# Gated cross-attention and mixture-of-experts blocks, one core: the stages before the first expert layer put in another order

## The reference

```python
def depool(h, ctx_n):
    s = scan(s = a * s + b * ctx_n[:, :256])
    return s[plug] + h

h = rmsnorm(layernorm(x)) * g_res @ W_in + b_in
x = x + tanh(g_xattn[0]) * depool(h, rmsnorm(ctx) * g_init)
x = x + tanh(g_ffn[0]) * moe_top1(layernorm(x))
x = x + tanh(g_xattn[1]) * attention(layernorm(x), ctx)
x = x + tanh(g_ffn[1]) * moe_top2(layernorm(x))
```

## Time and profile before

| | us |
|---|---|
| three runs of the kernel before: median | 1360.92 |
| lowest and highest | 1360.55, 1364.99 |
| the profiled execution, its own time | 1368.55 |
| its span, first to last instruction | 1366.8 |
| busy in the span: PE, PEld | 1180.5, 863.4 |
| busy in the span: DVE, ACT, POOL | 520.4, 465.5, 479.6 |
| mean granted TensorE clock | 0.932 |

### The profile page before, as it was taken

How to read it: one execution, slowest core, us unless ns; L and a number is a source line. 1 busy time by engine, 2 the same in 40 slices (tenths; PEclk the granted TensorE clock), 3 DMA queues, 4 the chain that set the end, 5 groups by cost and what they waited for, 6 DMA issues and landing times.

```text
span 1366.8 us, 19293 instructions
## 1 busy us (share of the span) xinstructions
PE 1180.5 (86%) x7110; PEld 863.4 (63%) x7110; DVE 520.4 (38%) x1256; ACT 465.5 (34%) x1067; POOL 479.6 (35%) x496
## 2 busy tenths in 40 slices
PE   2466799999995889999999999999948999998986
PEld 2246699999993444545445454434438888888875
DVE  1574322221114796767667676522060010000100
ACT  2111122221110245555555555663302333333331
POOL 0150111111113156767557675580002333333322
PEclk9885699999996689999999999999957999999998
DMA  6114487878862000000000000012005999999984
GB/s 202 50 62 154 170 292 277 292 291 305 325 251 100 0 1 1 1 17 1 1 1 17 1 1 16 9 39 101 0 0 196 317 306 315 294 308 302 330 299 124
DMA packets 53978, 197.18 MB, mean 144 GB/s; under 512 B 8539, under 2 KB 34397, under 8 KB 38013
## 3 DMA queue, kind: packets, MB, share of 16 engines
q1 hardware_dynamic: 39584, 173.35, 35.7%
q0 software_dynamic: 10464, 18.36, 5.5%
q10 hardware_dynamic: 3836, 4.24, 1.0%
HBM read 179.54 MB, written 16.38 MB: 143 GB/s over the span
## 4 chain that ended last, share of the span: by engine, by line
PE 66%; DMA 14%; DVE 10%; issue 4%; ACT 3%; POOL 1%; SPq 1%; ACTq 0%; POOLq 0%; DVEq 0%
PE PQ L394 16%; DMA out<-Z,SI 10%; PE PB L408 10%; PE PB L499 7%; PE PQ L484 7%; PE PB L468 5%; PE PQ L538 4%; PE PB L279 4%; PE PB L489 4%; DVE Z L872 3%; PE PQ L468 2%; DMA Z<-xn,SI 2%; PE PB L359 2%; DVE SM L585 1%; PE PQ L279 1%
## 5 line engine op out<-in xcount | busy, mean ns | idle before, releaser
L394 PE MATMUL PQ<-Z,WS 128*128 128x128 f32 x2720 | 329.4, 278 | 13.7 <-issue 12.6
L394 PEld LDWEIGHTS PQ<-Z,WS 128*128 128x128 f32 x2720 | 324.6, 194 | 26.1 <-issue 19.6
L408 PE MATMUL PB<-WS,Z 128*128 128x256 f32 x992 | 237.1, 383 | 0.0
L872 DVE TENSOR_REDUCE Z<-PB 128x1 f32<-128x402 f32 x340 | 183.4, 567 | 87.1 <-PE PB L468 85.8
L408 PEld LDWEIGHTS PB<-WS,Z 128*128 128x128 f32 x992 | 180.6, 192 | 19.9
L484 PE MATMUL PQ<-QS,KS 128*128 128x512 f32 x416 | 173.1, 437 | 7.3 <-ACT Z L1082 4.5
L1020 ACT ACTIVATE Z<-PQ,WS 128x128 f32<-128x128 f32 x312 | 88.9, 368 | 208.7 <-PE PQ L394 208.7
L468 PE MATMUL PB<-KS,QS 128*128 128x402 f32 x340 | 132.6, 402 | 15.6 <-DVE Z L872 6.8
L484 PEld LDWEIGHTS PQ<-QS,KS 128*128 128x128 f32 x416 | 77.1, 190 | 105.0 <-issue 60.8
L1082 ACT ACTIVATE Z<-PQ 128x512 f32<-128x512 f32 x208 | 109.7, 604 | 86.2 <-PE PQ L484 86.0
L1082 ACT ACTIVATE WS<-PQ 128x512 f32<-128x512 f32 x208 | 109.3, 605 | 80.6 <-PE PQ L484 80.6
(11 more groups left out here) (242 smaller groups left out, 1213.1 us busy)
## 6 DMA issues: line engine op xcount, KB each, us to landing
WS<-in_w SPq DMA_DIRECT2D x62, 1024.0 KB, 6.7
WS<-in_w SPq DMA_DIRECT2D x23, 2048.0 KB, 7.9
WS<-in_w SPq DMA_DIRECT2D x39, 1028.0 KB, 7.5
Z<-in_b SPq DMA_DIRECT2D x39, 128.0 KB, 6.7
xn<-WS SPq DMA_DIRECT2D x32, 128.0 KB, 1.7
X<-in_x SPq DMA_DIRECT2D x4, 512.0 KB, 10.7
WS<-yd SPq DMA_DIRECT2D x4, 512.0 KB, 5.5
out<-X SPq DMA_DIRECT2D x4, 512.0 KB, 2.9
```

The source lines that it names most:

```text
L394: t = e.matmul(bank[:, j * P:j * P + P], w[:, k, o:o + P], FXT[i % 2][:, k * P:k * P + P], start=k == 0, stop=k == 1)
L408: t = e.matmul(y, FS[c % 4][:, j * P:j * P + P], w[:, 4 * n + j, :], start=n == 0 and j == 0, stop=n == 1 and j == 3)
L872: e.tensor_reduce(MP[j % 2][:, i:i + 1], PB[bank_of["pc", r]][:, 0:PIECE], AX.X, ALU.max).then_inc(v_pc, 1)
```

## The change

- The x side comes first. Its statistics are taken while the sums of squares are still being made, right behind `v_loh`. Both norms of x are one power: the product of the two is (var (1 + eps) + eps^2)^-0.5.
- The right half of the context is loaded by SP's queue behind x; the small loads are split in six that are needed first (`d_first`) and six others (`d_small`). ScalarE issues constants, left half and the zero stores, makes the 13 left squares, then the 13 right ones, and then `Tanh`. The squares are written to WS[0] in place of PSUM.
- A list `mixed`, read by TensorE and VectorE, sets the order: x blocks 0 to 3, then two depool blocks and one x block in turn, then x blocks 10 to 15. Depool uses PSUM banks 2 and 3, so it no longer shares 6 and 7 with the projection. The projection goes straight into X, scaled by the gate (`projected`); the rows of g_init and b_in are scaled by the gate once, so that depooled rows are gathered ready scaled.
- DG has 16 buffers. A gather waits for the landing of the fourth one before it, no longer for X.
- One loop on VectorE adds the gathered rows to X, takes statistics, and five blocks behind normalizes for the router. The power is taken in four groups of four columns, between the gathers on GpSimd.

The diff is indented by 8 columns less than the code. Left out of it are the declaration of `v_h0`, and the later powers, whose numbers go up by two.

```diff
-DG = [WS[1][:, 2048 + 256 * i:2304 + 256 * i] for i in range(4)]
+DG = [WS[1][:, 2048 + 256 * i:2304 + 256 * i] for i in range(NC)]
...
-d_plen, d_x, d_cst, d_ctx, d_small = (sem(n) for n in ("d_plen", "d_x", "d_cst", "d_ctx", "d_small"))
+d_plen, d_cst, d_ck, d_v, d_first, d_small = (sem(n) for n in ("d_plen", "d_cst", "d_ck", "d_v", "d_first", "d_small"))
+d_x = [sem(f"d_x{g}") for g in range(4)]
...
+
+mixed = [("x", c) for c in range(4)]
+for c in range(NK):
+    mixed += [("dep", c)] + ([("x", 4 + c // 2)] if c % 2 else [])
+mixed += [("x", c) for c in range(10, NC)]
+
...
-    for c in range(NK):
-        bank = PB[6 + c % 2][:, 0:D]
+    def turn_h(c):
+        e.wait_ge(v_hin, c + 1)
+        if c >= 2:
+            e.wait_ge(a_ht, c - 1)
+        e.transpose(PB[4 + c % 2][:, 0:P], HIN[c % 4][:, 0:P], ident)
+        e.transpose(PB[4 + c % 2][:, P:2 * P], HIN[c % 4][:, P:2 * P], ident).then_inc(t_hin, 1)
+
+    def project(b):
+        e.wait_ge(a_ht, b + 1)
+        if b == 0:
+            e.wait_ge(v_win, 2)
+        if b >= 2:
+            e.wait_ge(v_h0, b - 1)
+        e.matmul(PB[6 + b % 2][:, 0:D], HT[b % 4][:, 0:P], Win[:, 0, :], start=True, stop=False)
+        e.matmul(PB[6 + b % 2][:, 0:D], HT[b % 4][:, P:2 * P], Win[:, 1, :], start=False,
+                 stop=True).then_inc(t_h, 1)
+
+    def depool(c):
+        bank = PB[2 + c % 2][:, 0:D]
         e.wait_ge(v_u, c + 1)
+        if c == 0:
+            e.wait_ge(v_cn, 1)
         if c >= 2:
             e.wait_ge(v_dep, c - 1)
         t = e.matmul(bank, CT[:, C_L:C_L + P], U3[c % 3], start=True, stop=c == 0)
...
             t = e.matmul(bank, CT[:, C_L2:C_L2 + P], U3[(c - 1) % 3], start=False, stop=True)
         t.then_inc(t_dep, 1)
 
-
-    for c in range(NC + 2):
-        if c < NC:
-            e.wait_ge(v_hin, c + 1)
-            if c == 0:
-                e.wait_ge(v_cn, 1)
-                e.wait_ge(a_ss, 2 * NK)
-            if c >= 2:
-                e.wait_ge(a_ht, c - 1)
-            e.transpose(PB[4 + c % 2][:, 0:P], HIN[c % 4][:, 0:P], ident)
-            e.transpose(PB[4 + c % 2][:, P:2 * P], HIN[c % 4][:, P:2 * P], ident).then_inc(t_hin, 1)
-        b = c - 1
-        if 0 <= b < NC:
-            e.wait_ge(a_ht, b + 1)
-            if b == 0:
-                e.wait_ge(v_win, 2)
-                e.wait_ge(v_dep, NK)
-            if b >= 2:
-                e.wait_ge(v_x1, b - 1)
-            e.matmul(PB[6 + b % 2][:, 0:D], HT[b % 4][:, 0:P], Win[:, 0, :], start=True, stop=False)
-            e.matmul(PB[6 + b % 2][:, 0:D], HT[b % 4][:, P:2 * P], Win[:, 1, :], start=False,
-                     stop=True).then_inc(t_h, 1)
+    for kind, c in mixed:
+        if kind == "dep":
+            depool(c)
+        else:
+            turn_h(c)
+            if c:
+                project(c - 1)
+            if c == NC - 1:
+                project(c)
 
 
     for c in range(NC + 1):
...
         if 0 <= b < NC:
             e.wait_ge(a_xt, b + 1)
             if b == 0:
-                e.wait_ge(v_x1, NC)
+                e.wait_ge(v_h0, NC)
+                e.wait_ge(d_small, 96)
             e.matmul(PB[6][:, b * E:b * E + E], XT[b % 4][:, 0:P], rw0s[:, 0:E], start=True, stop=False)
             e.matmul(PB[6][:, b * E:b * E + E], XT[b % 4][:, P:2 * P], rw0s[:, E:2 * E], start=False,
                      stop=True).then_inc(t_lg, 1)
...
+
+    for c in range(NC):
+        if c % 4 == 0:
+            e.wait_ge(d_x[c // 4], 16)
+        stats(c)
+    e.wait_ge(vc.sem, vc.n)
+    e.tensor_scalar(rst2, var, 1.0 + EPS, EPS * EPS, ALU.mult, ALU.add).then_inc(v_pw, 1)
+
...
-    e.wait_ge(d_ctx, 80)
-    e.wait_ge(a_ss, 2 * NK)
-    vc.step(e, e.tensor_tensor(rs, ssk, ssv, ALU.add))
-    e.tensor_scalar(rs, rs, 1.0 / (2 * D), EPS, ALU.mult, ALU.add).then_inc(v_pw, 1)
+    e.wait_ge(d_first, 96)
+    for k in range(2):
+        e.tensor_scalar(Win[:, k, :], Win[:, k, :], gres[:, k:k + 1], None, ALU.mult).then_inc(v_win, 1)
     e.wait_ge(p_pw, 1)
-    vc.step(e, e.tensor_scalar(rs, rs, float(np.float32(np.exp(-0.001))), None, ALU.mult))
+
+    def scaled(c):
+        if c >= 4:
+            e.wait_ge(t_hin, c - 3)
+        e.tensor_scalar(HIN[c % 4], X[:, c, :], mean[:, c:c + 1], rst2[:, c:c + 1], ALU.subtract,
+                        ALU.mult).then_inc(v_hin, 1)
+
+    def projected(b):
+        e.wait_ge(t_h, b + 1)
+        e.scalar_tensor_tensor(X[:, b, :], PB[6 + b % 2][:, 0:D], tg[:, 0:1], X[:, b, :], ALU.mult,
+                               ALU.add).then_inc(v_h0, 1)
 
     def evac_dep(c):
         e.wait_ge(t_dep, c + 1)
         if c >= 2:
             e.wait_ge(d_dep[c % 2], landed(c - 2, 2))
-        e.tensor_tensor(DR[c % 2], PB[6 + c % 2][:, 0:D], bIB, ALU.add).then_inc(v_dep, 1)
-
-    e.wait_ge(d_small, 176)
-    for c in range(NK):
-        if c >= 3:
-            e.wait_ge(t_dep, c - 1)
-        e.scalar_tensor_tensor(U3[c % 3], CK[:, c, :], rs[:, c:c + 1], gIB, ALU.mult, ALU.mult).then_inc(v_u, 1)
-        if c >= 1:
-            evac_dep(c - 1)
-    evac_dep(NK - 1)
-
-
-    e.wait_ge(d_x, 64)
-    for c in range(NC):
-        stats(c)
-    inv_std()
-    e.wait_ge(p_pw, 2)
-    vc.step(e, e.tensor_tensor(rst2, rst, rst, ALU.mult))
-    vc.step(e, e.tensor_tensor(rst2, rst2, var, ALU.mult))
-    e.tensor_scalar(rst2, rst2, EPS, None, ALU.add).then_inc(v_pw, 1)
-    e.wait_ge(p_pw, 3)
-    vc.step(e, e.tensor_tensor(rst2, rst2, rst, ALU.mult))
-    for k in range(2):
-        e.tensor_scalar(Win[:, k, :], Win[:, k, :], gres[:, k:k + 1], None, ALU.mult).then_inc(v_win, 1)
-    for c in range(NC + 2):
-        if c < NC:
-            if c >= 4:
-                e.wait_ge(t_hin, c - 3)
-            e.tensor_scalar(HIN[c % 4], X[:, c, :], mean[:, c:c + 1], rst2[:, c:c + 1], ALU.subtract,
-                            ALU.mult).then_inc(v_hin, 1)
-        b = c - 2
-        if 0 <= b < NC:
-            e.wait_ge(t_h, b + 1)
-            e.wait_ge(d_dg[b % 4], landed(b, 4))
-            if b == 0:
+        e.tensor_tensor(DR[c % 2], PB[2 + c % 2][:, 0:D], bIB, ALU.add).then_inc(v_dep, 1)
+
+    for kind, c in mixed:
+        if kind == "x":
+            scaled(c)
+            if c == 2:
                 e.wait_ge(a_tg, 1)
-            vc.step(e, e.tensor_tensor(DG[b % 4], PB[6 + b % 2][:, 0:D], DG[b % 4], ALU.add))
-            e.scalar_tensor_tensor(X[:, b, :], DG[b % 4], tg[:, 0:1], X[:, b, :], ALU.mult,
-                                   ALU.add).then_inc(v_x1, 1)
-            e.wait_ge(v_x1, b + 1)
-            stats(b)
+                for row_of in (gIB, bIB):
+                    vc.step(e, e.tensor_scalar(row_of, row_of, tg[:, 0:1], None, ALU.mult))
+            if c >= 2:
+                projected(c - 2)
+        else:
+            if c == 0:
+                e.wait_ge(a_ss, 2 * NK)
+                vc.step(e, e.tensor_tensor(rs, ssk, ssv, ALU.add))
+                e.tensor_scalar(rs, rs, 1.0 / (2 * D), EPS, ALU.mult, ALU.add).then_inc(v_pw, 1)
+                e.wait_ge(p_pw, 2)
+                vc.step(e, e.tensor_scalar(rs, rs, float(np.float32(np.exp(-0.001))), None, ALU.mult))
+            if c >= 3:
+                e.wait_ge(t_dep, c - 1)
+            e.scalar_tensor_tensor(U3[c % 3], CK[:, c, :], rs[:, c:c + 1], gIB, ALU.mult,
+                                   ALU.mult).then_inc(v_u, 1)
+            if c >= 1:
+                evac_dep(c - 1)
+        if (kind, c) == ("x", 10):
+            evac_dep(NK - 1)
+    projected(NC - 2)
+    projected(NC - 1)
 
     def route(l, rb, nt, logits):
         picks = 1 + l
...
-    inv_std()
-    e.wait_ge(p_pw, 4)
-    for c in range(NC):
-        if c >= 4:
-            e.wait_ge(t_xn, c - 3)
-            e.wait_ge(d_xn[0][c % 4], landed(c - 4, 4))
-        e.tensor_scalar(XN[c % 4], X[:, c, :], mean[:, c:c + 1], rst[:, c:c + 1], ALU.subtract,
-                        ALU.mult).then_inc(v_xn, 1)
+    e.wait_ge(v_h0, NC)
+    for b in range(NC + 5):
+        if b < NC:
+            e.wait_ge(d_dg[b % 4], landed(b, 4))
+            e.tensor_tensor(X[:, b, :], DG[b], X[:, b, :], ALU.add).then_inc(v_x1, 1)
+            e.wait_ge(v_x1, b + 1)
+            stats(b)
+            if b % 4 == 3:
+                inv_std(b - 3, b + 1)
+        c = b - 5
+        if c >= 0:
+            e.wait_ge(p_pw, 3 + c // 4)
+            if c >= 4:
+                e.wait_ge(t_xn, c - 3)
+                e.wait_ge(d_xn[0][c % 4], landed(c - 4, 4))
+            e.tensor_scalar(XN[c % 4], X[:, c, :], mean[:, c:c + 1], rst[:, c:c + 1], ALU.subtract,
+                            ALU.mult).then_inc(v_xn, 1)
...
 @block.scalar
 def _(e):
     e.dma_start(CT, cst).then_inc(d_cst, 16)
-    e.dma_start(CK[:, 0:12, :], ctx_2048[0:12 * P, 0:D].rearrange("(c p) d -> p c d", p=P)).then_inc(d_ctx, 16)
+    e.dma_start(CK[:, 0:12, :], ctx_2048[0:12 * P, 0:D].rearrange("(c p) d -> p c d", p=P)).then_inc(d_ck, 16)
     e.wait_ge(v_pad, 2)
```

(63 more changed lines are left out.)

19 lines of the change are left out of this document (10 added, 9 removed).

## The result

| us | before | changed |
|---|---|---|
| median, runs of one chip | 1361.14 (1360.55 to 1364.99, 4 runs) | 1329.33 (1326.43 to 1332.34, 4 runs) |
| ratio, 95% interval | | 0.9746, 0.9720 to 0.9772 |
| profiled execution, span | 1368.55, 1366.8 | 1326.77, 1325.0 |
| routing starts | 130.00 | 93.20 |

What follows compares the result with a forecast made beforehand. The bound was one serial path ahead of routing, at 130.00 us. Start -4.3, middle -37.3, gathers and router +7.6 make -34.0: routing at 96.0 and, from the median 1360.92, 1326.9 us; range 1317 to 1340.

Steps and rivals of the forecast that it cites:

- case A: The forecast itself: TensorE paces the mixed loop at 2.4 GHz, GpSimd paces the end; 1326.9 us; chance 0.82.
- Part 1: Start: reordered loads, squares before Tanh, one merged power; first depool operand at 37.2 against 41.45, 4.3 us won.
- The terms listed for the range: Lower: clock -2, adds -1, loads -1, faster router -3.6, spread 3, 1317; upper: turned round, table +1.3, 1340.
- Part 2: Mixed loop of depools and x blocks: TensorE the bound, 3.1 us a round, projections done at 65.2; middle -37.3 us.
- The clock's term: Start and mixed loop: clock low until about 38, then high; low until 42 costs 2 us, high from 30 gives 2.
- Rival B: Mixed loop: clock stays at 1.2 GHz, a round takes 6.1 us, 26 us more, 1353; chance 0.09.
- Part 3: Gathers and router in one loop: GpSimd's pace, 6.16 us a group; routing at 96.0, stage 7.6 us worse.
- rival C: Start, gathers: later context, adds 0.8 us, gathers 4.5 us to landing; 7 to 9 more, 1335; chance 0.04.
- Rival D: Gathers: VectorE's adds of two SBUF tiles slow GpSimd's; gain gone from 3.7 us a gather, 1367 at 4.1; chance 0.02.
- Rival E: Router: last six blocks run at 2.4 GHz and cost half, 3.6 us less, 1323; chance 0.02.
- Downstream: Behind the router: first expert's weight load stays hidden; routing, experts and attention unchanged and only shift.
- signs of being wrong: Mixed loop's clock at 0.5, gathers over 2 us apart, squares awaited beyond 30, or later stages changing over 4 us.

Runs made afterwards that it cites:

- Experiment 1: Changed kernel with Tanh and its wait for the small loads put back ahead of the squares on ScalarE: 1338.23 us, ratio 0.9817.
- experiment 9: Kernel before, with only the wait for the small loads, the zero stores and Tanh moved behind the squares: 1362.35 us, ratio 0.9981.
- experiment 3: Changed kernel with one power of 16 columns behind all gathers and the router only after it: 1337.84 us, ratio 0.9801.
- experiment 5: Changed kernel with added matmuls that nobody reads, keeping TensorE busy through router, ranks and tables: 1332.48 us, ratio 0.9748.
- experiment 4: Changed kernel with the 13 depool blocks in one piece behind x blocks 0 to 3, then x blocks 4 to 15: 1334.96 us, ratio 0.9789.
- The changed kernel's second profile: Changed kernel run again without an edit, beside the last two trials: 1329.19 us, ratio 0.9750.
- experiment 6: Changed kernel with a second, unread power of 16 columns on GpSimd at the start: 1328.94 us, ratio 0.9742.
- experiment 2: Changed kernel with four buffers for the gathered rows instead of sixteen: 1326.87 us, ratio 0.9732.

## Why the prediction was right

**Sign, mechanism and size** came out as case A says: 1329.33 against 1326.9 us, inside the range. Routing was to gain 34.0 us and gained 36.8. That the time is only 2.4 us off is partly luck: the path came out 2.8 us better than forecast, and the median moved 5.0 us less than the path. The parts, each against its own step:

| step, us | forecast | measured |
|---|---|---|
| squares done, V half | 28.5 | 27.1 |
| first depool operand | 37.2 | 34.6 |
| round of two depools and one x block | 3.1 | 3.01 |
| first gather | 59.4 | 56.95 |
| last projection done | 65.2 | 62.1 |
| first power of four columns | 70.2 | 66.4 |
| last gather | 83.7 | 80.4 |
| routing | 96.0 | 93.2 |

*Part 1* holds with terms too large. A square was priced at 0.47 us from the earlier trace rows; here they follow each other in 0.40. That counts for the 13 of the V half alone, 0.9 us, since they start at V's landing (21.77, I had 22.4) and not behind the K half, which ends at 20.9. The table load is not in the chain either: it ends under ScalarE's wait for the K half. VectorE waited 1.2 us for the last square, before 17.6. Experiment 1 measures the queue order at 7.7 us of routing, and experiment 9 shows that without the new loads it gives 2.2. One sum of Part 1 is off: 34.5 + 0.4 + 2.46 + 0.2 is 37.6 and not 37.2, which would make routing 96.4 and the time 1327.3. These last three terms took 3.0 us here, as priced. The terms listed for the range give 1316 to 1338 and not 1317 to 1340; the measured time lies in both.

*Part 2* holds in its main claim, TensorE's pace in the mixed loop: busy 26.35 of 26.50 us, 3.01 a round. The clock's term was off: I had it low to about 38, and the chain shows it up by 31 (a pair of matmuls takes 1.22 at 27.47, 0.66 at 29.98, 0.45 at 30.64). So the two projections and their evacuations ahead of the first operand took 4.1 us instead of 5.1, which is most of the rest of Part 1's error. Rival B falls in all eleven executions of the new order: none stayed at 1.2 GHz in the loop. But its premise was not empty: two of them lost 2.3 and 2.6 us to a low clock around the first depool (experiments 3 and 5), and in experiment 4 it was 0.72 in 46 to 52. That the mix counts and not just the overlap is what experiment 4's +5.5 us say, of which the clock may have made up to 1.7.

*Part 3* holds in its pattern and is off in two terms that nearly cancel. The groups of the changed kernel by form, and GpSimd's timeline:

```profile
L794 DVE TENSOR_TENSOR X<-WS,X 128x256 f32<-128x256 f32 x16 | 6.6, 413 | 1.9 <-DMA WS<-dep_d,SI 1.8
```
```profile
66.44 1.15 POOL L1155 TENSOR_TENSOR SM<-SM 128x4 f32<-128x4 f32 x1 [0.61 <-DVE SM L605]
67.79 1.02 POOL L1165 DMA_INDIRECT WS<-dep_d,SI  x1 [0.20 <-issue]
...
72.59 1.09 POOL L1155 TENSOR_TENSOR SM<-SM 128x4 f32<-128x4 f32 x1
73.84 1.03 POOL L1165 DMA_INDIRECT WS<-dep_d,SI  x1 [0.16 <-issue]
```

I took 0.59 us for the add, from another add of two SBUF tiles; it took 0.413, close to the lower bound of 0.45. Four blocks were therefore added in 4.1 us, not 4.7. Against that, a group of four gathers and a power takes 6.05 us (67.79 to 73.84) and then 6.59 (73.84 to 80.43) instead of 6.16, the powers 1.09 to 1.17 instead of 1.03, and the slow gather of the chain (4.67 us to its landing) cost VectorE 1.3. That slow landing was in Part 3 only as rival C's worst case, from the maximum of 4.5 in the earlier trace rows; it is no rare case, as the last section shows. From the last projection to routing it is 31.1 us, forecast 30.8. Without the split powers it is 10 more (experiment 3).

*Rival D* falls: with the adds of two SBUF tiles beside them, gathers are busy 0.95 to 1.19 us each, 1.01 in the mean against 0.96 before. The sharing of SBUF interfaces that the Trainium skill states (GPSIMD Engine Reference, Specifications) costs a gather no more than 0.04 us in these rows. Whether the powers' 1.09 to 1.17 us in place of 1.03 come from it, no run here shows. *Rival E* falls in this kernel, by the 0.50 of its last two stages.

*Downstream* nothing moved, as forecast, but one of my own signs of being wrong came up: a stage behind that changes by over 4 us. The last tiles were 5.4 shorter. The changed kernel's second profile has 298.4, and no kernel of the study edits them, so the range over all kernels points to the spread of executions, without telling what makes it.

*The sum.* On the path I was 2.8 us too pessimistic. The median moved by 31.8 us in the first comparison and by 34.8 in the last, which is 5.0 and 2.0 less than routing did. Both intervals (2.2 to 2.8%, so 31 to 38 us) hold the 36.8, so I take the difference as spread, which was not resolved further. To go by the median rather than the profiled execution was right: its 7.4 us above are in part the long last tiles.

**How the 36.8 us divide.** Experiments 1, 3, 6 and 2 each take one part back in the changed kernel: the order on ScalarE 7.7 us, the split powers 10.1, the merge of the two norms 0.1, the buffers 0. The largest part, depools and projections in one loop with the gathers beside it, was not undone as a whole. If the parts added up, 19 us would be left for it, and experiment 4 has up to 5.5 of them depend on the mix. But that they add up is not shown: the order on ScalarE alone gains 2.2 us in the kernel before (experiment 9), not 7.7.
